# A transformer layer with windowed attention and routed experts on one core: fp32 products as three fp32r passes, and a finer order of work

## What is computed

```python
x = x + attention(layernorm(x))      # 16 heads of 16, causal, window of 64 keys, fp32
x = x + ffn(layernorm(x))
# ffn: scores = sigmoid(xf @ gate_w.T + lb_bias); top 2 of 8 experts per token
#   expert e: silu(xf @ gate.T) * (xf @ up.T) @ down.T    (inner size 128)
#   its rows are multiplied by the mean weight of the tokens that chose e
#   plus one shared expert with inner size 256
```

## Time and profile before

| | |
|---|---|
| median of 3 runs | 613.49 us |
| the profiled execution's own time | 616.98 us |
| its span, first to last instruction | 615.2 us |
| granted TensorE clock, mean | 0.968 |
| TensorE busy | 555.0 us (90%) |
| VectorE busy | 354.0 us (58%) |
| ScalarE busy | 289.5 us (47%) |
| GpSimd busy | 218.4 us (36%) |
| mean DMA rate | 83 GB/s |

### The profile page before, as it was taken

How to read it: one execution, slowest core, us unless ns; L and a number is a source line. 1 busy time by engine, 2 the same in 40 slices (tenths; PEclk the granted TensorE clock), 3 DMA queues, 4 the chain that set the end, 5 groups by cost and what they waited for, 6 DMA issues and landing times.

```text
span 615.2 us, 14456 instructions
## 1 busy us (share of the span) xinstructions
PE 555.0 (90%) x4969; PEld 417.2 (68%) x4969; DVE 354.0 (58%) x1084; ACT 289.5 (47%) x650; POOL 218.4 (36%) x384
## 2 busy tenths in 40 slices
PE   7699999989898898898898987898999999999995
PEld 4466766666566565565575664786888887868884
DVE  4456577666465575675665567268555554533454
ACT  3366665645445555455455563221555554541110
POOL 4000012342240431422413423662456555555620
PEclk9899999999798998999999999698999999999999
DMA  7400000210201101112101101115455554518753
GB/s 249 164 3 3 2 2 4 62 45 20 63 23 40 52 20 55 37 27 63 36 2 38 36 2 38 70 57 159 135 152 162 153 159 134 157 58 301 247 147 126
DMA packets 37862, 50.79 MB, mean 83 GB/s; under 512 B 9244, under 2 KB 28063, under 8 KB 37792
## 3 DMA queue, kind: packets, MB, share of 16 engines
q1 hardware_dynamic: 31264, 33.02, 17.7%
q0 software_dynamic: 6528, 16.86, 8.3%
HBM read 27.36 MB, written 23.27 MB: 82 GB/s over the span
## 4 chain that ended last, share of the span: by engine, by line
PE 71%; DVE 13%; another core or an unknown queue 6%; ACT 4%; issue 3%; DMA 2%; POOL 1%; DVEq 0%; SPq 0%; POOLq 0%; ACTq 0%
PE ps L774 10%; PE ps L694 7%; PE ps L525 6%; PE ps L491 5%; PE ps L791 5%; PE ps L576 5%; PE ps L511 5%; PE ps L501 4%; DVE rmax L997 4%; PE ps L704 3%; PE ps L554 3%; PE ps L562 3%; PE ps L536 3%; PE ps L766 2%
## 5 line engine op out<-in xcount | busy, mean ns | idle before, releaser
L997 DVE TRANSPOSE_TENSOR_REDUCE rmax<-ps 128x32 f32<-128x1024 f32 x64 | 79.5, 1242 | 62.8 <-PE ps L525 61.0
L459 POOL DMA_INDIRECT y_rows<-vm,dest x72 | 70.2, 976 | 63.5 <-issue 40.1
L367 POOL TENSOR_TENSOR rstd<-mv,epsb 128x2 f32<-128x2 f32 x32 | 6.2, 193 | 241.6 <-DVE mv L982 241.6
L868 ACT ACTIVATE probs<-ps 128x1024 f32<-128x1024 f32 x64 | 65.7, 1026 | 25.0 <-PE ps L541 25.0
L774 PE MATMUL ps<-wF,wA 128*128 x288 | 75.0, 383 | 0.5 <-DVE wA L1246 0.5
L422 POOL DMA_INDIRECT z_slots<-z,slot x64 | 64.7, 1011 | 29.4 <-issue 18.0
L525 PE MATMUL ps<-bd,kT 64*128 64x256 f32 x512 | 66.4, 380 | 0.0
L694 PE MATMUL ps<-zT,wF 128*128 128x256 f32 x256 | 62.4, 388 | 0.6 <-ACT vm L957 0.6
L874 ACT COPY pvs<-ps 128x256 f32<-128x256 f32 x64 | 23.8, 372 | 81.5 <-remote 42.5
L694 PEld LDWEIGHTS ps<-zT,wF 128*128 128x128 f32 x256 | 49.5, 195 | 7.8 <-ACT vm L957 1.0
L525 PEld LDWEIGHTS ps<-bd,kT 64*128 64x128 f32 x512 | 50.0, 191 | 5.0
(11 more groups left out here) (160 smaller groups left out, 1095.5 us busy)
## 6 DMA issues: line engine op xcount, KB each, us to landing
z<-z_slots SPq DMA_DIRECT2D x72, 129.0 KB
bd<-y_rows SPq DMA_DIRECT2D x8, 512.0 KB, 7.4
out<-xs SPq DMA_DIRECT2D x16, 256.0 KB, 3.6
wF<-wffn SPq DMA_DIRECT2D x10, 384.0 KB, 3.3
xs<-x SPq DMA_DIRECT2D x7, 512.0 KB, 6.0
shift<-negs SPq DMA_DIRECT2D x128, 2.0 KB
z<-y_rows SPq DMA_DIRECT2D x4, 512.0 KB, 6.7
probs<-y_rows SPq DMA_DIRECT2D x4, 512.0 KB, 7.5
```

Source lines behind the costliest of these rows:

```text
L459: eng.indirect_dma_start(y_rows, bass.IndirectOffsetOnAxis(ap=dest[:, m:m + 1], axis=0), yo[:, m, :], None, bounds_check=K * T - 1, oob_is ...
L868: eng.activation(probs[:, n % 2, :], S[n % 2].rearrange("p a c -> p (a c)"), ACT.Exp, scale=HD ** -0.5).then_inc(s_P, 1)
L997: eng.tensor_reduce(rmax[:, n % 2, 0:32], S[n % 2].rearrange("p a (c q) -> p (a c) q", q=32), AX.X, ALU.max, apply_transpose=True).then_in ...
```

## The change

1. A helper `product` replaces one fp32 matmul by three matmuls on operands of type float32r: hi x hi, hi x lo, lo x hi. `hi` is a copy of the value as float32r, `lo` the difference. It is used for q, k, v, the output projection, gate and up (shared and in tiles) and the tiles' down product. The shared down product stays one fp32 matmul, with a weight tile `wD` of its own. Scores, values, shifts and transposes stay as they were.
2. So each such operand needs two copies: `hi` by ScalarE out of PSUM, `lo` by VectorE (PSUM minus hi). This holds for yT, zT, oT (four per group), the tiles' rows and hidden rows, and all weights (attention weights in the prologue, the ten weight blocks of the feed-forward part in groups 2 to 12 of the sweep, each by one copy of 128x768 on ScalarE and two subtractions of 128x384 on VectorE). The copy of the tiles' rows moves from VectorE to ScalarE, with the subtraction on VectorE.
3. `zT` is no longer kept for 16 groups: each group's hi and lo (512 KB) are stored to DRAM by SyncE in block n = 1, and loaded again into five places ahead of its gate and up products, by SyncE and ScalarE.
4. In `step`, `shift_of(b)` moves from behind the values product and the first projection product to right behind the scores of b+1; on ScalarE the exponential moves ahead of the copy of the values' output.
5. The router's logits are taken with moving operands of 16 columns (hi and lo weights side by side), summed by a reduction; the bias is one more operation in the ranking.
6. The order between sweep and tiles is finer (half a `gate_up` before the last output projection, the last logits two units earlier), and the tile table is computed with tiles on partitions (operations of 128x8 and 128x1) and spread by products with a matrix of ones.
7. At the end, `combined` is spread over the units by a list of turns, so that only the last one or two follow the last unit.

```diff
+                def product(out, lhsT, rhs, start, stop, skip=False):
+                    for n, (a, b) in enumerate(((0, 0), (0, 1), (1, 0))):
+                        mm = eng.matmul(out, lhsT(a), rhs(b), start=start and n == 0,
+                                        stop=stop and n == 2, skip_group_check=skip)
+                    return mm
...
-                            mm = eng.matmul(bank(BANK_A)[:, m, :], wA[:, 0, k, m * P:(m + 1) * P], yT[:, k, :],
-                                            start=k == 0, stop=k == KT - 1)
+                            mm = product(bank(BANK_A)[:, m, :], lambda a: wA[:, a, 0, k, m * P:(m + 1) * P],
+                                         lambda b: yT[:, b, k, :], k == 0, k == KT - 1)
...
@@ step, TensorE
                             scores_of(b + 1, par2, n2, mask_first if first else window_mask)
+                        shift_of(b, g, n)
                         if n == 1:
                             eng.wait_ge(s_v, g + 1)
                         if old or n:
...
-                        shift_of(b, g, n)
...
@@ epilogue, TensorE
+                    pvT_of(BPG * NG - 1)
                     logits_of(NG - 2)
                     oT_of(BPG * NG - 1)
+                    eng.wait_ge(s_wFl, 2 * NW)
+                    eng.wait_ge(s_wD, 16)
+                    gate_up(0, (0,))
                     eng.wait_ge(s_lg, NG - 1)
                     wo_of(NG - 1)
+                    gate_up(0, (1,))
+                    gate_up(1)
+                    places_of(NG - 2)
                     gate_up(2)
+                    zT_of(NG - 1, GPB - 1)
                     down(0)
+                    gate_up(3, (0,))
+                    logits_of(NG - 1)
...
@@ step, ScalarE
+                        exp_of(b, n, old == 0)
                         if old or n:
                             pv_copy(b - 1)
-                        exp_of(b, n, old == 0)
...
+                        if n == 3 and 2 <= g < NW + 2:
+                            w = g - 2
+                            eng.wait_ge(s_wf[w % 2], 16 * (w // 2 + 1))
+                            eng.copy(wF[0][:, weights_at(w), :], wraw_of[:, w % 2, :]).then_inc(s_wFh, 1)
...
@@ tile, ScalarE
+                    if not (last and m >= 6):
+                        rows_hi(*later(q, m, 2))
                     if not (last and m == 7):
                         silu(*later(q, m, 1))
-                    hidden_copy(*later(q, m, 0))
+                    hidden_hi(*later(q, m, 0))
...
@@ VectorE
+                def lo_of(dst, hi, src_bank, s_in, s_out, G):
+                    eng.wait_ge(s_in, G + 1)
+                    eng.tensor_tensor(dst, ps[:, src_bank, :].rearrange("p (a c) -> p a c", a=2), f(hi),
+                                      ALU.subtract).then_inc(s_out, 1)
...
@@ step, VectorE
+                        if n == 0 and old >= 2:
+                            lo_of(zT[:, 1, :, :], zT[:, 0, :, :], BANK_B, s_zTh, s_zTl, g - 2)
...
+                        if n == 2 and 3 <= g < NW + 3:
+                            split_weights(g - 3, 0)
...
+                        if n == 3 and ahead == 2:
+                            lo_of(yT[:, 1, :, :], yT[:, 0, :, :], BANK_A, s_yTh, s_yTl, g + 2)
...
+                        if old or n:
+                            oT_lo(b - 1, (n - 1) % BPG)
...
+                        if n == 3 and 3 <= g < NW + 3:
+                            split_weights(g - 3, 1)
...
@@ step, SyncE
+                        if n == 1 and old >= 2:
+                            store_zt(g - 2)
...
+                turn_of = [max(5 * g // 4 + 3, 2 * (g - GA) + 3) for g in range(NG)]
+                for n in range(NS * (NG - GA)):
+                    hidden_of(NS * GA + n)
+                    if n % 2 and n > 1:
+                        accumulate(GA + (n - 3) // 2)
+                    for g in range(NG):
+                        if turn_of[g] == n:
+                            combined(g)
```

More of the change, by code:

```diff
@@ L17 @@
 F32 = mybir.dt.float32
+F32R = mybir.dt.float32r
 I32 = mybir.dt.int32
@@ L146, in layer @@
         zin = z[:, :, :, :].rearrange("p g t c -> p (g t) c")
-        table = [probs[:, i, 0:NTS * E].rearrange("p (t e) -> p t e", e=E) for i in range(2)]
+        fit, fit_tiles = probs[:, 0, 0:E], probs[:, 0, E:2 * E]
+        e_col, start_col, off_col, row_col, w_col = (probs[:, 0, 16 + i:17 + i] for i in range(5))
+        diag = [probs[:, 0, 64 + NTS * i:64 + NTS * (i + 1)] for i in range(3)]
         esc = probs[:, 0, 640:640 + NT * E].rearrange("p (t e) -> p t e", e=E)
@@ L168, in layer @@
         s_id, s_const = sem("identity_loaded"), sem("constants_loaded")
-        s_wf = sem("ffn_weights_loaded")
+        s_wf = [sem(f"ffn_weights_loaded_{i}") for i in range(2)]
         s_pool = sem("pool_setup")
@@ L300, in epilogue @@
                 def epilogue():
-                    pass
+                    eng.wait_ge(s_S, BPG * NG)
+                    eng.wait_ge(s_zst, 32)
+                    for g in range(2):
+                        eng.dma_start(f(zt_of[g][0]), zT_dram[g].rearrange("p (a k c) -> p a k c", a=2, k=KT)
+                                      ).then_inc(zt_of[g][1], 16)
+                    store_zt(NG - 2)
+                    store_zt(NG - 1)
+                    eng.wait_ge(s_zst, 16 * NG)
                 sweep(eng, step, prologue, epilogue)
@@ L587, in logits_of @@
                     if 0 in tiles:
[L588 removed]
+                        eng.wait_ge(s_zTl, G + 1)
                     for t in tiles:
                         for k in range(KT):
[L591 to L592 removed]
+                            for a in range(2):
+                                mm = eng.matmul(ps[:, BANK_B, 16 * t:16 * t + 16], zT[:, a, k, t * P:(t + 1) * P],
+                                                wG[:, a, k, :, :].rearrange("p a e -> p (a e)"),
+                                                start=(k == 0 and a == 0), stop=(k == KT - 1 and a == 1))
                     if TPG - 1 in tiles:
@@ L737, in epilogue @@
                     places_of(NG - 1)
+                    down(2)
+                    gate_up(5)
+                    eng.wait_ge(s_dg, 1)
+                    eng.matmul(ps[:, BANK_B, 64:64 + 2 * NTS], onesf[:, :], probs[:, 0, 64:64 + 2 * NTS],
+                               start=True, stop=True).then_inc(s_tb, 1)
+                    down(3)
                     gate_up(6)
@@ L790, in tile_down @@
                     after(eng, s_y1, t - 1)
-                    eng.matmul(ps[:, 2 + m % 2, 0:D], hT[:, m % 2, :], weights(e, 4 * P, 6 * P), start=True, stop=True
-                               ).then_inc(s_d1, 1)
+                    product(ps[:, 2 + m % 2, 0:D], lambda a: hT[:, m % 2, a, :],
+                            lambda b: weights(e, b, 4 * P, 6 * P), True, True).then_inc(s_d1, 1)
                 def tile(q, m, first, last):
@@ L1166, in tile_table @@
                 def tile_table():
-                    chain(eng.tensor_tensor(table[0], const("tile").unsqueeze(2).to_broadcast([P, NTS, E]),
-                                           over_tiles(tiles_end), ALU.is_ge))
-                    chain(eng.tensor_reduce(tile_e[:, :], table[0], AX.X, ALU.add))
-                    chain(eng.tensor_tensor(table[0], table[0], over_tiles(tiles), ALU.mult))
-                    chain(eng.tensor_reduce(tile_w[:, :], table[0], AX.X, ALU.add))
+                    chain(eng.tensor_scalar(fit, tiles_end, const("index"), None, ALU.is_le))
@@ new lines, in tile_table @@
+                    chain(eng.tensor_reduce(e_col, fit, AX.X, ALU.add))
+                    chain(eng.tensor_tensor(fit_tiles, fit, tiles, ALU.mult))
+                    chain(eng.tensor_reduce(start_col, fit_tiles, AX.X, ALU.add))
+                    chain(eng.tensor_scalar(off_col, start_col, const("index"), -1.0 * P, ALU.subtract, ALU.mult))
+                    chain(eng.tensor_scalar(row_col, e_col, 1.0 * REGION, off_col, ALU.mult, ALU.add))
+                    eng.tensor_scalar(diag[0], identf[:, 0:NTS], e_col, None, ALU.mult)
@@ L1327 @@
         "quad": p[:, None] // HD % QH == np.arange(QH),
+        "index": p[:, None],
     }
```

396 lines of the change are left out of this document (240 added, 156 removed).

## The result

The changed kernel took 622.7 us (median of 4 runs, 619.9 to 627.2) beside 614.0 us for the kernel before on the same chip: a ratio of 1.015, 95% interval 1.008 to 1.022. It is 1.5% slower, where 587 us was forecast. The profiled execution took 620.9 us, its span 619.1.

A forecast was written before the change was run, and what follows sets the result against it. TensorE was taken to bound tiles and end in full, less so the sweep and the stage after it. 616.98 - 18 - 9 - 2.3 - 4.5 + 3 + 4 = 590.2, less 3.5 for the median: 587 us, range 561 to 616.

The forecast's parts named there:

- The bound of 11 to 22 us: Tiles: range of the saving, 22 us if TensorE alone sets the pace, 11 us at 1.48 us per tile.
- Price of a pass: All split products: a product of three float32r passes costs 0.33 us, 0.10 less than one fp32 product.
- Tiles: Tile stage: 1.38 us per tile with three engines close, TensorE's own sum 1.32; 18 us less.
- Units: End units: each falls from 2.59 to 2.18 us, 22 units, 9 us less; zT loads cost nothing.
- Behind the last unit: End of the kernel: with combined moved, only one or two additions are left; 2.3 us less.
- Between sweep and tiles: Stage before the first tile: the last scatter's chain ends last, output projection two units earlier; 4.5 us less.
- Start: Before the first maxima: VectorE's weight and yT subtractions, partly beside waits for loads; 4 us more.
- Sweep: Sweep groups: TensorE's saving of 1.6 us per group taken back by shift waits and VectorE's subtractions; 3 us more.
- the shift's landing: Sweep: the earlier shift leaves 1.4 us for a landing of 1.7; wait about 0.2 us per block, 0.8 per group.
- A: Rival on the passes: records of products lie 0.2 us apart instead of 0.11; chance 0.08.
- B: Rival in the sweep: the shift's DMA takes TensorE's place, slower than before, 635 us at 2.6 us landing; chance 0.10.
- C: Rival in the sweep: it keeps TensorE's saving, 26 + 3 us less, 560 us; chance 0.12.

The follow-up runs named there:

- a_plain_again: Changed kernel with scatters spread over the group's blocks and the tiles' stores as plain DMAs, on a chip with hold-ups: 578.0 us, ratio 0.937.
- r1: Changed kernel with the table's matmul behind down(3) and gate_up(6), and hidden_of(4) ahead of the table, on a chip without hold-ups: 563.3 us, ratio 0.974.
- t1: Changed kernel with ScalarE's copy of the next rows one place earlier, ahead of the scaling, on a chip without hold-ups: 561.9 us, ratio 0.969.
- f1: Changed kernel with each product as one plain fp32 matmul of the high halves: 597.1 us (1.031) without hold-ups, 627.6 us (1.018) with them.
- t1r1: Changed kernel with the edits of t1 and r1 together, on a chip with hold-ups: 629.0 us, ratio 1.025.
- o1: Changed kernel with only the first of each product's three passes, on a chip without hold-ups: 526.8 us, ratio 0.909.
- mix: Changed kernel with spread scatters, r1's edits, the earlier kernel's tiles and unsplit expert weights, only shared blocks split; no hold-ups: 567.8 us, ratio 0.979.
- a_plain_stores: Changed kernel with scatters spread over the group's blocks and the tiles' stores as plain DMAs, on a chip without hold-ups: 562.9 us, ratio 0.971.
- b_spread_turns: Kernel before with spread scatters and the changed kernel's turns of combined at the end, on a chip without hold-ups: 574.7 us, ratio 0.990.
- b_spread: Kernel before with the four scatters of a group spread over its four blocks, on a chip with hold-ups: 584.8 us, ratio 0.947.

## Why the prediction was wrong

**The step that failed** is in the tiles: "With three engines that close I take 1.38 us per tile: 72 x 0.25 = 18 us less." I listed TensorE, ScalarE, VectorE and GpSimd's time per store (0.98 + 0.30) and took the fullest. What sets the tiles on this chip is none of them but how close the indirect stores come. At 1.63 us apart they passed (1.69 us on average, with a few longer tiles), at 1.41 they do not, and the average becomes 1.81 to 1.85; as plain stores they pass again, at 1.55 (a_plain_again). The bound of 11 to 22 us had no case below zero, so the range could not hold the result. The prediction had the hold-up before its eyes in the earlier trace rows and wrote: "The hold-up in groups with scatters (ScalarE stands 3.9 us, TensorE 2.4) I leave as it is, since the scatters stay." It did not ask what triggers it and whether the tiles, which issue an indirect DMA each, come nearer to that.

**Where the chip has no hold-ups the sign is the forecast's.** There r1 and t1 took 563.3 and 561.9 beside 578.7, 2.6 to 3.1% less, with neither of their edits moving its stage; the changed kernel itself never met such a chip. That is 15 to 17 us less, against 26 forecast. Term by term, r1's stages against the kernel with spread and turns on such a chip (whose end I add back as 2.9 us):

- *Price of a pass*: the sum takes 0.33 us per product, 0.10 less than before, that is 0.11 us per pass; no row and no run shows that term. The chain of waits of the changed kernel shows 0.12 us per pass, 0.36 per product, 0.07 less.
- *Tiles*: 107.0 against 114.7, 8 us instead of 18. A pass of 0.12 us makes TensorE's sum 0.22 + 0.72 + 0.11 + 0.36 = 1.41, not 1.32, and once in eight tiles 0.6 us are added (0.9 in t1), seen here in r1's chain of waits:

```profile
432.57 0.11 PE ps L850
432.68 0.36 PE ps L520 x3
433.04 0.22 PE ps L833 x2
433.26 0.72 PE ps L520 x6
433.98 0.19 issue
434.17 0.30 PE ps L850
434.50 0.62 PE ps L520 x3
```

  It stands where the changed kernel loads eight registers at once ahead of the hidden row's transpose (before, four and four). That the loading is the cause I read from its place; it was not tried, and f1, which loads the same eight, shows only 0.1 to 0.2 us in the same place.
- *Units*: 55.8 against 62.6, 6.8 us instead of 9, the measured pass again: 2.30 us per unit, not 2.18. The loads of zT never stopped TensorE, here or on the first chip, where the DMA engines moved 320 GB/s at a share of 0.87 from 562 to 609 us; the 283 GB/s that I had measured them against was no limit.
- *Behind the last unit*: 2.9 us instead of 2.3.
- *Between sweep and tiles*: nothing gained (50.5 against 49.9) instead of 4.5. I took the last scatter as what ends last, but the scatter came 1 us earlier and the first tile did not: TensorE's units with the three waits for the table, the sums and the weight column in between last as long. On the first chip it is 4.7 us worse. TensorE stands 2.47 us at L616 for ScalarE's copy, where t1 has 0.50. Then VectorE goes on 2.4 us late behind the scatters ahead of the last counts, all of the table is behind it, and TensorE stands 3.75 us in order, where t1 has 1.65. These two make 4.1 us of it:

```profile
411.00 0.18 DVE L1189 TENSOR_TENSOR slots<-ps,cst 128x16 f32<-128x16 f32 x1 [2.36 <-remote]
...
415.24 0.85 PE L800 MATMUL ps<-probs,onesf 128*128 128x144 f32 x2 [3.75 <-issue]
```

  Moving L800 alone (t1r1, 55.6 us) mends nothing there, as the next wait takes its place. What would mend it stays open.
- *Start*: 0.2 us instead of 4 in this execution, 0.5 to 1.9 in three later ones of the changed kernel; the new subtractions lie beside the loads' waits.
- *Sweep*: nothing saved in all, as forecast (361.6 against 362.2), and in the main for the reason given: VectorE has little room. o1 shows it best, and mix puts the splits at 0.5 us per group (forecast 0.3). The other half of the reason, the shift's landing, was wrong: TensorE's load ahead of L595 waited for it 11.9 us in all, 5.9 of that once at the start, which leaves 0.1 us per block. (The prediction's own 1.7 less 1.4 is 0.3, where it took 0.2.) Moving it back costs 37 us.

**The rivals.** A (records 0.2 us apart) is refuted: passes that load 128x128 weights each start 0.12 us apart, twelve in 1.44 us. B (slower, by the shift's DMA) had the sign and not the mechanism. C (the sweep keeps TensorE's saving) came in part only. Groups 1 to 3, ahead of the first scatters, take 19.08, 20.05 and 20.19 us, before 20.16, 20.87 and 20.87: they keep 0.7 to 1.1 us of the 1.1 that 16 products save. Over the whole sweep f1 shows that 13 us of passes were saved and 12 us of new work spent.

## What to carry to other kernels

When an edit makes a loop faster, look at everything the loop issues, not at the engines' sums alone: a resource that was just good enough at the old pace can turn the sign. With the scatters spread in both kernels the change still loses 17 us on a chip with hold-ups (601.9 against 584.8); with its stores made plain as well it is at 578.0 on another such chip (ratio 0.937). A wait in the trace whose sender was long done is a question to be settled before the forecast, not a constant; here spreading four scatters over a group gave 5% on a chip that has it (584.8 us, ratio 0.947) and cost nothing measurable on one that has not (sweep 326.6 us in a_plain_stores, 327.9 in r1). And a verdict of 1 or 2% from one chip may not be one for the next: b_spread_turns is below the kernel before on both kinds as far as run (0.990 without hold-ups; with them its near twin b_spread, 0.947), while the changed kernel's variants win without hold-ups (0.97) and the changed kernel loses with them (1.010 to 1.016).

## What the hardware showed

- Three of the five sets of runs, and the first comparison, were on chips where other engines go on late, with waits of up to 3.9 us, when scatters are issued 1.3 us apart, and where tiles with indirect stores 1.41 us apart take 1.81 to 1.85 us. At 1.63 us apart, or as plain stores, tiles take 1.69 and 1.55 us. On the chips of the other two sets no trace has such a wait. Which part of the chip is held up is not shown by these traces. Each of the five sets had a chip of its own, so it is likely, but not shown, that the chip and not the moment makes the difference.
- A float32r pass (one load of 128x128 weights, 256 columns) takes 0.12 us in a row of passes (twelve in 1.44 us), three of them 0.36 against 0.43 for one fp32 matmul.
- The loads of the experts' rows take 10.8 us instead of 7.4 beside the loads of zT, at 0.87 of the DMA engines' time, and no unit waits for it; with the zT loads cut they land after 8 us and the units take 55.8 us, as in r1.
